# Output and layer 1 of one graph and the front of the next, spread as units into the attention slots of the graph between

## The reference

```
h = relu(layernorm(x));  Q, K, V = proj(Wq, bq), proj(Wk, bk), proj(Wv, bv)    # 8 heads of 32
scores = einsum('bhnd,bhmd->bhnm', Q, K) * SCALE;  scores = where(adj == 0, -inf, scores)
out = einsum('bhnm,bhmd->bhnd', softmax(scores), V)
x = x + einsum('bno,po->bnp', out, Wo) + bo
h = relu(layernorm(x))
e_k = leaky_relu(einsum('bid,bjd->bij', h * a_k[:, 0], h), 0.2)                # k = 0 to 3
scores = e_0 where adj == 1, e_1 where 2, e_2 where 3, e_3 where 4, else -9e15
x = x + einsum('bij,bjd->bid', softmax(scores), h)
```

## Time and profile before

| | |
|---|---|
| runs of the kernel | median 3982.55 us of 3 (3978.19 to 3991.47) |
| span of the profiled execution | 3976.3 us |
| PE busy | 3669.7 us, 92% |
| DVE busy | 3128.6 us, 79% |
| ACT busy | 2267.1 us, 57% |
| POOL busy | 674.9 us, 17% |
| chain that ended last | PE 68%, SP queue 11%, issue 9%, DVE 7% |

### The profile page before, as it was taken

How to read it: one execution, slowest core, us unless ns; L and a number is a source line. 1 busy time by engine, 2 the same in 40 slices (tenths; PEclk the granted TensorE clock), 3 DMA queues, 4 the chain that set the end, 5 groups by cost and what they waited for, 6 DMA issues and landing times.

```text
span 3976.3 us, 94630 instructions
## 1 busy us (share of the span) xinstructions
PE 3669.7 (92%) x34096; PEld 2908.9 (73%) x34096; DVE 3128.6 (79%) x5926; ACT 2267.1 (57%) x3940; POOL 674.9 (17%) x440
## 2 busy tenths in 40 slices
PE   6989989899998989989899898998989989899998
PEld 5777777777777767777777777776777767777776
DVE  6968778687886978869788696886968869688785
ACT  3837547275573845738456384663836638366482
POOL 1021030310303103031020301203012030120300
PEclk8999999999999999999999999999999999999999
DMA  5041220403204032040310503104031040311300
GB/s 151 2 105 36 60 82 2 117 25 70 71 2 118 23 76 66 2 131 10 81 61 4 137 2 83 59 15 126 2 89 53 21 121 2 95 47 31 99 2 12
DMA packets 129070, 227.67 MB, mean 57 GB/s; under 512 B 20672, under 2 KB 71104, under 8 KB 128448
## 3 DMA queue, kind: packets, MB, share of 16 engines
q1 hardware_dynamic: 128448, 219.50, 20.3%
HBM read 101.98 MB, written 16.78 MB: 30 GB/s over the span
## 4 chain that ended last, share of the span: by engine, by line
PE 68%; SPq 11%; issue 9%; DVE 7%; DMA 2%; ACT 1%; DVEq 0%; POOL 0%; POOLq 0%; ACTq 0%
PE pT L856 21%; PE ps L837 15%; PE pO L873 13%; SPq L220 11%; PE ps L773 8%; PE pO L975 7%; PE pT L908 2%; DMA adj_half<-in_adj_dram 2%; PE pT L963 2%; DVE pt L525 1%; DVE most L483 1%; DVE sm L667 1%; PE pO L884 1%; DVE sm L510 1%; DVE sm L674 1%
## 5 line engine op out<-in xcount | busy, mean ns | idle before, releaser
L349 ACT ACTIVATE sm<-sm,mn 128x1024 f32<-128x1024 f32 x1024 | 1179.5, 1152 | 454.8 <-DVE mn L510 452.5
L510 DVE CUSTOM_DVE_ANT_0 sm<-ps,bias 128x1024 f32<-128x1024 f32 x1024 | 1250.9, 1223 | 197.5 <-PE ps L837 178.0
L856 PE MATMUL pT<-ident,sm 128*128 128x128 f32 x8192 | 1098.6, 276 | 40.3 <-DVE pt L525 37.1
L856 PEld LDWEIGHTS pT<-ident,sm 128*128 128x128 f32 x8192 | 961.3, 142 | 218.5 <-DVE pt L525 52.8
L837 PE MATMUL ps<-ks,qs 96*128 96x512 f32 x2048 | 754.4, 451 | 4.6 <-issue 3.7
L525 DVE COPY pt<-pT 128x512 f32<-128x512 f32 x1024 | 702.4, 686 | 31.5 <-PE pT L856 30.8
L873 PE MATMUL pO<-pt,v 128*32 128x128 f32 x16384 | 649.7, 278 | 4.8 <-DVE pt L525 4.8
L359 ACT COPY pt<-pT 128x512 f32<-128x512 f32 x1024 | 583.2, 570 | 56.7 <-PE pT L856 56.4
L290 POOL TENSOR_SCALAR bias<-adj_half 128x512 bf16<-128x512 int32 x240 | 468.0, 1950 | 864.3 <-DMA adj_half<-in_adj_dram 855.7
L873 PEld LDWEIGHTS pO<-pt,v 128*32 128x32 f32 x16384 | 388.2, 109 | 170.1 <-issue 170.1
L975 PE MATMUL pO<-h,pt 128*128 128x256 f32 x2048 | 463.0, 379 | 0.0
(11 more groups left out here) (104 smaller groups left out, 3526.5 us busy)
## 6 DMA issues: line engine op xcount, KB each, us to landing
adj_half<-in_adj_dram SPq DMA_DIRECT2D x256, 256.0 KB, 2.8
ks<-pt SPq DMA_DIRECT2D x384, 128.0 KB, 2.4
qs<-pt SPq DMA_DIRECT2D x384, 128.0 KB, 2.4
xf<-in_x_dram SPq DMA_DIRECT2D x16, 1024.0 KB, 8.0
x<-in_x_dram SPq DMA_DIRECT2D x16, 1024.0 KB, 5.7
out_dram<-x SPq DMA_DIRECT2D x128, 128.0 KB, 2.9
x<-in_L_gnn_Wq_dram SPq DMA_DIRECT2D x1, 256.0 KB, 2.8
x<-in_L_gnn_Wk_dram SPq DMA_DIRECT2D x1, 256.0 KB, 3.1
```

The lines of the kernel that those rows point to most:

```text
L349: nc.scalar.activation(sm[:, t % RING, :], sm[:, t % RING, :], ACT.Exp, scale=-1.0, bias=mn[:, t:t + 1], accum_out=den[:, t:t + 1]).then_i ...
L510: nc.vector.tensor_tensor_reduce(out=sm[:, t % RING, :], in0=ps[t % 2][:, :], in1=bias[:, node, :], scale=1.0, scalar=3e38, op0=ALU.add, o ...
L856: last = nc.tensor.transpose(pT[c][:, j * P:(j + 1) * P], sm[:, t % RING, m * P:(m + 1) * P], ident[:, :])
```

## The change

There is now one stage per graph, its 64 attention slots. Into them go units: v and the second half of q and k of the graph itself (slots 1, 2, 4, 6), output, h transposes and the eight edge tiles of the graph before (slots 3, 5, 10, 11, and 13, 17, ... 41), and the front and the first half of q and k of the next graph (53, 55, 57, 58). A unit fills a whole bank `ps`; score tiles and units take the two banks in turn (`score_banks`), and TensorE waits with each for the eviction of what stood there. Output and v are evicted as halves of 1024 columns. An edge tile's transposes and copies stand three slots later, its values as two halves in the two slots after the next edge tile, with one probability buffer (`pt[:, HG]`), one pB and the fourth `sm`.

`pt` holds one group of four tiles and layer 1's; `values` of a group runs whole at the next slot divisible by four, ahead of its transposes. One accumulator pA serves attention, pB the rows, the edge values and the flag. The row factors are made in `ot`, transposed to pB; ScalarE copies pA over them and `norm` multiplies by pB; h1 shares memory with xf, and the scaled parts ah and al of h with the parts of q and k. ah and al are made for all of h at once.

The adjacency of a graph is loaded twice, once for its masks and once as `gbias`, tile by tile, for layer 1 (`edge_bias` on POOL, `edge_adj` on SP). The flag's maximum leaves VectorE: POOL sums max(adj - 1, 0) over all halves in `over`, so that a mask half is three POOL operations, and VectorE reduces `over` once. The mask of node block n of the next graph waits for mask tile 32 + 4 * (n + 1). The normalisation of h goes to ScalarE alone. The first graph has no earlier part, the last stage no later one, and output and layer 1 of the last graph follow alone. The diff, cut to its core (SP's, POOL's, ScalarE's, VectorE's, then TensorE's part):

```diff
-SLOTS = 8
...
+def background(earlier, later):
+    units = {1: ("value", 0), 2: ("value", 1), 4: ("qk", 2), 6: ("qk", 3)}
+    if earlier:
+        units.update({3: ("out", 0), 5: ("out", 1), 10: ("h", 0), 11: ("h", 1)})
+        units.update({13 + 4 * t: ("edge", t) for t in range(NT)})
+    if later:
+        units.update({53: ("front", 0), 55: ("front", 1), 57: ("qk", 0), 58: ("qk", 1)})
+    return units
+def score_banks(units):
+    slots, turn = {}, 0
+    for s in range(TILES):
+        slots["score", (s + 2) % TILES] = turn % 2
+        turn += 1
+        if s in units:
+            slots[units[s]] = turn % 2
+            turn += 1
+    assert turn % 2 == 0
+    return slots
+def ring(t):
+    return 3 if t == TILES - 1 else t % RING
...
-        h1 = sb("h1", [P, NT, D], F)
-        ot = h1[:, :, :].rearrange("p a b -> p (a b)").rearrange("p (k n) -> p k n", k=KT)
-        pt = sb("pt", [P, SLOTS, NT, P], F)
-        stage = pt[:, :, :, :].rearrange("p (q c) m n -> p q c (m n)", q=4).bitcast(R)
+        h1 = xf
+        ot = sb("ot", [P, KT, N], F)
+        gbias = sb("gbias", [P, N], BF)
+        parts = sb("parts", [P, 4, N], R)
+        ah = parts[:, 0:2, :]
+        al = parts[:, 2:4, :]
+        sm = sb("sm", [P, RING + 1, N], F)
+        pt = sb("pt", [P, HG + 1, NT, P], F)
...
-        pO = [ctx.enter_context(nc.psum_tensor(f"pO{i}", [P, HALF], F)) for i in range(2)]
+        pA = ctx.enter_context(nc.psum_tensor("pA", [P, HALF], F))
+        pB = ctx.enter_context(nc.psum_tensor("pB", [P, HALF], F))
...
+                if later:
+                    mask_adj(b + 1, 1, base)
+                    mask_adj(b + 1, 2, base)
+                store(o, 6)
+                if later:
+                    mask_adj(b + 1, 3, base)
+                    sp.wait_ge(pv, NT * (o + 1))
+                    settle(sp)
+                    load_xf(b + 1, 0)
+                    load_xf(b + 1, 1)
+                store(o, 7)
+                if later:
+                    mask_adj(b + 1, 4, base)
+                sp.wait_ge(y_out, 16 * NT * (o + 1))
+                settle(sp)
+                load_x1(b)
+                if later:
+                    mask_adj(b + 1, 5, base)
+                    mask_adj(b + 1, 6, base)
+                    sp.wait_ge(s_mm, TILES * b + TILES // 2)
+                    settle(sp)
+                    first_stack(b + 1, (0, 1))
+                    mask_adj(b + 1, 7, base)
+                    stack_heads(b + 1, (2, 3))
...
+            def masks(f, node, loaded):
+                for c in range(2):
+                    half = bias[:, node, c * HALF:(c + 1) * HALF]
+                    made = 2 * NT * f + 2 * node + c + 1
+                    pool.wait_ge(adj_in[c], 16 * (loaded + 1))
+                    settle(pool)
+                    if node == 0 and c == 0:
+                        nc.gpsimd.tensor_scalar(over[:, :], adj_half[:, c, :], 1.0, 0.0, ALU.subtract,
+                                                ALU.max).then_inc(over_sum, 1)
+                    else:
+                        nc.gpsimd.tensor_scalar(half, adj_half[:, c, :], 1.0, 0.0, ALU.subtract,
+                                                ALU.max).then_inc(over_half, 1)
+                        pool.wait_ge(over_half, (2 * NT - 1) * f + 2 * node + c)
+                        pool.wait_ge(over_sum, made - 1)
+                        nc.gpsimd.tensor_tensor(over[:, :], over[:, :], half, ALU.add).then_inc(over_sum, 1)
+                        pool.wait_ge(over_sum, made)
+                        settle(pool)
+                    nc.gpsimd.tensor_scalar(half, adj_half[:, c, :],
+                                            0.0, BIG, ALU.is_equal, ALU.mult).then_inc(mask_made, 1)
+                    pool.wait_ge(mask_made, made)
+                    pool.sem_inc(adj_used[c], 1)
...
+                if later:
+                    next_masks(b + 1, 0)
+                    edge_bias(o, NT - 1, base + edge_load(NT - 1))
+                    for node in range(1, 5):
+                        next_masks(b + 1, node)
+                    front_norm(b + 1)
+                    next_masks(b + 1, 5)
+                    residual(b)
+                    next_masks(b + 1, 6)
+                    next_masks(b + 1, 7)
...
+            def copy(b, t, first):
+                act.wait_ge(tr[0], TILES * b + t + 1)
+                if t >= HG:
+                    act.wait_ge(av, GROUPS * b + t // HG)
+                elif not first:
+                    act.wait_ge(av, GROUPS * b)
...
+                for s in range(TILES):
+                    if s + 2 < TILES:
+                        mask(b, s + 2, banks["score", s + 2], not earlier)
+                    elif later:
+                        mask(b + 1, s + 2 - TILES, banks["score", s + 2 - TILES], False)
+                    kind, n = units.get(s, ("", 0))
+                    if kind == "value":
+                        value_add(b, n, banks["value", n], not earlier)
+                    if kind == "out":
+                        out_add(o, n, banks["out", n])
+                    if kind == "qk":
+                        qk_low(b if n >= 2 else b + 1, n, banks["qk", n])
+                    if kind == "h":
+                        h_low(o, n, banks["h", n])
+                    if kind == "edge":
+                        loaded = base + (edge_load(n) if later else n)
+                        select(o, n, banks["edge", n], loaded, general)
+                        edge_mask(o, n, banks["edge", n], loaded)
+                    if kind == "front":
+                        front_low(b + 1, n, banks["front", n])
+                    if earlier and 16 <= s < 16 + 4 * NT and s % 4 == 0:
+                        edge_copy(o, (s - 16) // 4)
+                    if earlier and 19 <= s < 19 + 4 * (NT - 1) and s % 4 == 3:
+                        result(o, (s - 19) // 4)
+                    if earlier and s == 45:
+                        result(o, NT - 1)
+                    copy(b, s, not earlier)
+                    if kind == "edge":
+                        edge_leaky(o, n)
+                    if s % 16 == 15:
+                        row_factors(b, s // 16, not earlier)
+                    if s == 0 and earlier:
+                        norm(o, QUADS - 1)
+                    if s and s % 16 == 0:
+                        norm(b, s // 16 - 1)
+                    if earlier and s in (3, 5):
+                        layer_stats(o, (s - 3) // 2)
+                    if earlier and s == 5:
+                        layer_aggregate(o)
+                    if earlier and s == 7:
+                        layer_shift(o)
+                    if earlier and s == 8:
+                        general = read_flag(o)
+                    if s == 20:
+                        flag_rows(b)
+                    if later and s in (48, 49):
+                        front_stats(b + 1, s - 48)
+                    if later and s == 49:
+                        front_aggregate(b + 1)
+                    if s == 52:
...
+                for s in range(TILES):
+                    if s + 2 < TILES or later:
+                        if s - 1 in units:
+                            pe.wait_ge(masked, TILES * b + s + 2)
+                        elif s - 2 in units:
+                            released(b, units[s - 2])
+                        else:
+                            pe.wait_ge(masked, TILES * b + s + 1)
+                        if s + 2 < TILES:
+                            scores(b, s + 2, banks["score", s + 2])
+                        else:
+                            scores(b + 1, s + 2 - TILES, banks["score", s + 2 - TILES])
+                    if s == 12 and earlier:
+                        general = read_flag(o)
+                    kind, n = units.get(s, ("", 0))
+                    if kind and s - 1 in units:
+                        released(b, units[s - 1])
+                    elif kind:
+                        pe.wait_ge(masked, TILES * b + s + 2)
+                    if kind == "value":
+                        value(b, n, banks["value", n])
+                    if kind == "out":
+                        out_product(o, n, banks["out", n])
+                    if kind == "qk":
+                        qk(b if n >= 2 else b + 1, n, banks["qk", n])
+                    if kind == "h":
+                        h_transposes(o, n, banks["h", n])
+                    if kind == "edge":
+                        if n == 0:
+                            pe.wait_ge(normed, QUADS * b)
+                        if n == 1:
+                            pe.wait_ge(normed, QUADS * b + 1)
+                        if n == 5:
+                            pe.wait_ge(normed, QUADS * b + 2)
+                        edges(o, n, banks["edge", n], general)
+                    if kind == "front":
+                        front_transposes(b + 1, n, banks["front", n])
```

(75 more changed lines are left out.)

1312 lines of the change are left out of this document (636 added, 676 removed).

## The result

Four runs of the changed kernel have a median of 4364.0 us (4358.59 to 4365.36), the kernel before 3987.0 beside them: ratio 1.0947, 95% interval 1.0917 to 1.0977. The forecast was 4200, at most 4320. The direction held, and so did most of the chain of waits; what released the front, and the size of several terms, did not.

The account below looks back on a forecast made before the run. TensorE was taken to bind, with VectorE 0.37 us behind per slot. Period 60.0 + 122.7 + 72.2 + 3.0 = 257.9 us; 584 + 14 x 257.9 = 4195, so 4200; range 3970 to 4320.

Parts of the forecast that it names:

- What bounds the kernel; the form of attention: TensorE binds before, VectorE only 0.37 us behind per slot; four slots without units then take 9.25 us, formerly 8.46.
- Slots 0 to 12: Units, evictions and copies wait for each other on two banks: 60.0 us against 47.5 of work.
- The wait for the front: After slot 45, mask 51 releases POOL's node 4; normalised rows at 31.3, TensorE arrives at 26.6: wait 4.7 us.
- Rival B: POOL's queue, not mask 51, sets node 4 (add 1.95, node 12.8); front's rows 5.4 later: 4275 us; chance 0.15.
- the main case: The summed chain of waits in head and tail: 4200 us, with 4090 to 4300 as its own; chance 0.51.
- The port of the memory: Two-SBUF-input VectorE and GpSimd operations exclude each other: 6 us on POOL's queue by the skill, hardly shown by the trace.
- From the front to the seam: From rows at 31.3, late copies and evictions, then SP's stacks; head 2 lands at 72.2, TensorE arrives at 68.4.
- The clock: Behind the waits of 4.7 and 3.8 us TensorE runs at 1.2 GHz; 3.0 us counted per period.
- The fixed parts: Outside the 14 full periods: start 61, first stage 189, last stage 229.7, last graph's output and layer 1 104.5 us.
- A: Faster: neighbouring slots cover evictions, TensorE binds throughout, stacks land in time; about 230 a period, 3790 us; chance 0.12.
- C: Only the head costs, POOL and stacks come in time: about 4010 to 4050 us; chance 0.14.
- D: The merged V saves nothing: 0.4 x 16 a period more, 4290 us; chance 0.04.

Follow-up runs that it names:

- clock_hold: Changed kernel with matmuls that nobody reads put ahead of the front transposes and of the seam's scores: 4405.8 us.
- adj_first: Changed kernel with the adjacency load of mask node 1 issued on SP ahead of the store of layer 1's tile 5: 4318.3 us.
- pool_short: Changed kernel with two of a mask half's three POOL operations, the sum for the flag, left out: 4225.0 us.
- norm_first: Changed kernel with the front's normalisation ahead of the mask of node block 4 in POOL's queue: 4291.4 us.

## Why the prediction was wrong in size

The sum had 4195 of span, the trace has 4362, 167 more. From the first flag to the last the sum has 14 x 257.9 + 251.7 = 3862 and the trace 3988, 126 more; the stage cut above has 265.7 for a period of 257.9, 7.8 more. Ahead of the first flag it has 61 + 46 + 74 + 26 = 207, and the flag stands at 222 (15 more). Behind the last it has 21 + 104.5 = 125.5, and there are 151.6 (26 more). These 7.8 are 4.0 in slots 0 to 12, 2.9 in 13 to 44 and 4.0 from slot 45 to the seam, less the 3.0 that the sum had entered apart for the clock.

- **What bounds the kernel; the form of attention: right.** 9.15 us for four free slots in the last stage (9.25 forecast); quads (four slots) with a layer 1 tile 15.2 (15.1), those with edges 1 and 5 16.4 and 16.5 (16.1), the edge transposes 0.5 behind the copy (0.45). The middle came out 125.6 against 122.7: 1.9 of the 2.9 stand in its first four slots, 16.3 where the sum has 14.4. TensorE waits there for a copy of ScalarE, a wait that the sum had not, and the lower clock follows it:

```profile
2209.96 1.06 PE L978 MATMUL pT<-ident,sm 128*128 128x128 f32 x8 [2.06 <-ACT pt L486]
2211.99 1.96 PE L1039 MATMUL pT<-ident,sm 128*128 128x128 f32 x8 [0.51 <-DVE pt L686]
```

- **Slots 0 to 12: the chain right, the clock not in it.** 64.0 against 60.0. The lower clock behind the seam's wait is 3.0 by clock_hold, and V of group 2, behind a wait of 2.85, takes 3.64 where 1.95 was in the sum. These 4.7 are more than the whole difference, 4.0. The h units were chained as forecast.
- **The wait for the front: the step that failed, 4.0 of the 7.8.** The sum let mask 51 release node 4, and put the front's rows at 31.3; they came at 35.3. Rival B, at 0.15, had the mechanism (the queue sets node 4) and 36.7 for the place, but for the wrong reason: the add takes 1.17, as the main case said (1.14), not 1.95. What pushed the queue was a DMA issue on SP, blocked by a store for tile 5, a line that the prediction named only as costing nothing, "since a POOL operation of 1.95 or more on the other half lies beside each load". Beside this load none lay. adj_first prices it at 46 us: there node 4 does wait for mask 51, begins at 16.9 (16.4 forecast), and the front's rows come at 32.5. The other 1.2 of the 4.0 are this mask, 0.5 late, and a node of 11.3 where 10.6 was taken.
- **The port of the memory: there, and nearly free, as the prediction weighed it.** Two rows of the last edge tile, VectorE's leaky operation first:

```profile
2317.09 1.22 DVE L790 SCALAR_TENSOR_TENSOR sm<-sm 128x1024 f32<-128x1024 f32 x1
2317.85 2.25 POOL L364 TENSOR_SCALAR bias<-adj_half 128x512 bf16<-128x512 int32 x1 [0.29 <-POOL bias L371]
```

  In the whole trace 14 of POOL's subtractions (L364) begin while a leaky operation runs, and 12 of them take 1.98 to 2.52 us; the 226 others take 1.92 to 1.94. What the 12 have more is what the leaky operation still has to run, less about 0.15. The other way round the leaky operations show nothing: 120 of the 128 begin while POOL makes a mask or an edge bias, and all take 1.21 or 1.22. But the one-column operation ahead of them (L788) takes 0.28 to 0.58 us in the 105 cases in which it begins within 0.34 us of the start of a POOL operation, and 0.15 or 0.16 in the 23 others; it ends about 0.6 us after POOL's start. The Trainium skill (SBUF — State Buffer, SBUF: two separate sides) lets a VectorE operation with two SBUF inputs and a GpSimd operation that reads SBUF shut each other out, the first to start for its whole length. The trace agrees that each holds the other up; GpSimd's hold of VectorE lasts about 0.6 of its 1.93 us here. POOL's 12 waits come to 2.8 us in 4362, so this is no part of the miss.
- **From the front to the seam: right.** 40.85 us against 40.9 forecast, with stacks landing about 2.4 after the last issue; head 2 is late, as said.
- **The clock: named, but mis-sized.** 3.0 a graph was taken. There are four V at 3.5 to 3.6 us a graph (groups 2, 12, 14, 15), 1.5 to 1.7 over full speed each, and transposes and scores beside them. The prediction counted only behind the two longest waits; waits of 2.6 and 1.45 in a row did the same, and V of group 14 came at granted clock 0.52 behind waits of 1.2, 0.45, 0.72 and 0.71. Not all of it reaches the end: V of groups 12 and 14 stand ahead of the waits for POOL and for the stacks. What shows is 3.0 behind the seam, 1.7 in V of group 2 and 0.9 behind the front, an estimate of 5.6 a graph.
- **The fixed parts: mis-sized.** A layer 1 tile alone was put at 7.9 us. In the last graph's layer 1, which follows alone, the transposes of the eight tiles start 9.8 to 11.7 apart:

```profile
4294.73 1.09 PE L1039 MATMUL pT<-ident,sm 128*128 128x128 f32 x8 [1.95 <-ACT sm L510]
4296.66 5.38 PE L1050 MATMUL pB<-xf,pt 128*128 128x256 f32 x16 [0.83 <-ACT pt L517]
...
4305.86 1.09 PE L1039 MATMUL pT<-ident,sm 128*128 128x128 f32 x8 [1.05 <-ACT sm L510]
```

The sum had TensorE never wait for the exponential; it waits ahead of six of the eight, 1.05 to 3.98, and the values behind that take 3.69 to 6.33 (3.3 was taken). Seven spacings of about 10.9 instead of 7.9 are 21 of the 26. The 15 at the start are POOL's length again, in the first graph, whose masks POOL makes one behind the other. VectorE waits 5.84 us there for a mask and then, in slot 20, for POOL's sum of the flag, with TensorE behind it both times (5.82 and 13.62):

```profile
141.61 0.69 DVE L711 TENSOR_REDUCE most_all<-over 128x1 f32<-128x512 bf16 x1 [12.65 <-POOL over L368]
144.41 1.11 PE L978 MATMUL pT<-ident,sm 128*128 128x128 f32 x4 [13.62 <-DVE pt L686]
```

In pool_short neither wait is there and the flag's matmul stands at 197.8, 24 earlier. The sum put nothing for this wait.

- **Rivals.** A falls: the period is 266, not below 241. C falls by norm_first, pool_short and adj_first, each of which finds a POOL cost that C did not have. D falls: V whole at 1.95 us is in every row at full clock. The range's upper end, 4320, rested on a period of 266 and kept the fixed parts as they were; the period reached it, and the 41 us of fixed parts stood outside. That the period came out at 266 is luck as far as that bound goes: it had an add of 1.95 us in it, and the add takes 1.17. The signs named as right are all there (a period of 266, C to C 1.75, both clusters of idle time, POOL at 1964 us), and the time is outside the range all the same: they tell the chain and not its sizes.

## What to carry to other kernels

Before an idle stretch is filled with units of other work, price, by itself, the form that the filling asks of the loop that takes it in: here one lump of V and one buffer group cost 6.4% with nothing filled, against 8% of idle time in all. For a step that is moved into a queue, follow the load of its input through the issuing queue as well, past every store that waits. And look first at what the idle time waits for: two loads moved ahead of 48 issues took 2.6% off the kernel before, with nothing else changed.

## What the runs showed of the hardware

- The granted clock fell to 0.50 inside a kernel that is over 80% busy, behind waits of 2 to 6 us and once behind four of 0.45 to 1.2, and a burst of 64 short matmuls showed it most: 3.64 us against 1.95, and a 512-column one 0.63 against 0.39. Filling two of the waits with matmuls raised the mean granted clock from 0.919 to 0.943.
- The turn of a loop on TensorE shows 2.2 to 3.7 us of idle time with nothing to wait for, and 2.2 to 3.2 more after the first matmul behind it (13 turns, 77.8 us), in the kernel that had independent work there; the same code outside the loop shows none. Where a wait for data stands at the turn, the pause cannot be told from it.
- POOL's time for 128x512 int32 to bfloat16 was 1.93 us, and for an add in bfloat16 1.17, as a quarter of the 128x2048 float32 add of the earlier trace rows would have it.
- A GpSimd operation that began during a VectorE operation with two SBUF inputs took up to 0.59 us longer (2.52 for 1.93). A VectorE operation of that kind that began within 0.34 us of GpSimd's start took 0.13 to 0.43 longer (0.28 to 0.58 for 0.15), one that began later took no longer.
